# Layer 1's head and the fourth maximum of layers 1 and 3 moved in a four-layer attention kernel; semaphores cleared by five engines

## The chip, the cores and the metric

The kernel runs on one core of one Trainium2 chip. The metric is the device time of one execution in microseconds (us); lower is better. The kernel before takes 4179.82 us in the median of three runs (4173.48 to 4180.5).

## What is computed

Four attention layers in a row on a batch of four, each with tensors of 512 tokens by 512 features in float32. Cut to what matters:

```
x = L0(x, ctx)          # layernorm, 16 heads of 32, softmax, projection, GELU MLP
x = L1(x, ctx, mask)    # 32 query heads of 16 on 8 key heads, additive 512x512 mask, layernorm behind
x = L2(x, ctx, mask)    # layernorm of ctx, 16 heads of 32, tanh-gated residual
x = L3(ctx, x, mask)    # x asks, concat(ctx, x) of 1024 keys answers, rmsnorm, GELU MLP
# in each: scores = q @ k.T (scaled, masked); attn = softmax(scores); out = attn @ v
```

## The kernel before, in words

One loop runs over the four batch elements; its body computes all four layers for one element with everything in on-chip memory. The body's work is a hand-written list, `STEPS`, built layer by layer in `layer_steps` (lines 99 to 184). Every engine walks the same list and takes the steps that concern it, so the list's order is the order of each engine's instructions; counting semaphores hold the engines together.

**Steps.** `q` and `k` project 128 features and split the result in a high and a low part (two ScalarE instructions, lines 937 to 944, one GpSimd subtraction, line 646), which SyncE's queue stacks into one operand by 2 to 4 transfers of 256 KB each (line 600). Both parts' buffers are used again by the next `q` or `k`: ScalarE may write them only when the last stacking has landed. `max` multiplies one block of queries with all 512 keys (TensorE line 779) and VectorE takes each row's maximum (line 1075 in layer 1, where the mask is added on the way; line 1078 in layer 3). `maxT` transposes a unit's maxima (line 790), VectorE splits them (lines 1089, 1090), and two small transfers write them as rows of the query operand (line 607); only then may that unit's first `score` start. `score` computes two banks of transposed scores (line 807; in layer 1 with two more matmuls each that add the mask, lines 810 and 811), ScalarE takes the exponential (line 950), `pv_half` and `pv` multiply the probabilities with values and with ones (lines 848 and 850; line 827 in layer 1). `heads` closes a unit: ScalarE and VectorE fetch numerators and sums (VectorE lines 1103 to 1120). A unit is a group of four heads; layer 1 has eight units of four key tiles, layer 3 four units of eight key tiles, in two halves of 512 keys. `emax` is the form of `max` that computes two blocks at once in the score banks ahead of the attention; `part` is one of the four pieces of a projection between which emaxes are put.

**Two ring banks.** Everything but scores and pv results goes through two PSUM banks in turn (`RING = 2`): a ring step may start on TensorE when the step two before it has been taken away by VectorE or ScalarE (`take_ring`).

**The order around the change.** In the attention part the list goes group by group, one group for each key tile of a unit. Each group holds two scores of the next group, its own pv, and a share `part` of the maxima of later units (`late`, spread by a running count, or in layer 3 by the table `plan`):

```
steps += part[0:1] + ahead[0:1] + part[1:2] + ahead[1:2] + part[2:3]
steps += ([("pv_half", n, u, kt)] if n != 1 else []) + [("pv", n, u, kt)]
if kt == L.kt - 1:
    steps.append(("heads", n, u))
steps += part[3:]
```

So three filling steps stand ahead of pv and the fourth (and a fifth) behind pv and behind `heads`. `k(3,3,0)` and `k(3,3,1)`, the last keys of layer 3, are the fourth step of their groups.

**End of an iteration.** Behind the loop body SyncE clears 43 semaphores one after the other (lines 1144, 1145), then all engines meet at a barrier (line 1146) and the next iteration starts.

Of the kernel before, what the change touches and what calls it, by code (L numbers as in the profile page):

```python
# [34 lines left out]
NT = S // P  # L35
NC = D // P
# [43 lines left out]
def in_parts(main, between, first):  # L80

    out, pieces, gap = [], iter(between), 0
    for step in main:
        for c in range(NC):
            out.append(("part", step, c) if c < NC - 1 else step)
            gap += 1
            if gap > first:
                out += next(pieces, [])
    return out + [s for piece in pieces for s in piece]


def spread(steps, first, last):

    count = last - first + 1
    cuts = [len(steps) * i // count for i in range(count + 1)]
    return {first + i: steps[cuts[i]:cuts[i + 1]] for i in range(count)}


def layer_steps(L):

    n = L.n
    pairs = [(u, j, t, h) for u in range(L.units) for j in range(4) for t in range(0, NT, 2) for h in range(L.halves)]

    def closes(u, j, t, h):
        return [("maxT", n, u)] if (j, t, h) == (3, NT - 2, L.halves - 1) else []

    def early(count):
        return [[("emax", n, *p)] + closes(*p) for p in pairs[:count]]

    def late(count):  # L110
        out = []
        for u, j, t, h in pairs[count:]:
            out += [("max", n, u, j, t, h), ("max", n, u, j, t + 1, h)] + closes(u, j, t, h)
        return out

    def q(u):
        return ("q", n, u)

    def k(u, h=0):
        return ("k", n, u, h)  # L120

    def v(t, layer=n):
        return ("v", layer, t)

    if n == 0:
        done = 16
        steps = [("ctxT", c) for c in range(NC)] + [("norm", 0, "x"), v(0), k(0), v(1)] + [("xT", 0, "z", c) for c in range(NC)]
        steps += in_parts([q(0), k(1), q(1), v(2), v(3), q(2), k(2), q(3), k(3)], early(done), 17)
    elif n == 1:
        done = 12  # L130
        steps = [("maskT", 0), ("maskT", 1)] + [("xT", 1, "x", c) for c in range(NC)] + [q(0), ("maskT", 2), ("maskT", 3)]
        steps += in_parts([q(1)] + [v(t, 3) for t in range(NT)], early(done), 8)
    elif n == 2:
        done = 16
        steps = [("aT", c) for c in range(NC)] + [("norm", 1, "out"), k(0), v(0), v(1)]
        steps += [("xT", 2, "x", c) for c in range(NC)]
        steps += in_parts([q(0), k(1), v(2), q(1), v(3), k(2), q(2), k(3), q(3)], early(done), 16)
    else:
        done = 32
        steps = [k(0)] + [("xT", 3, "x", c) for c in range(NC)]  # L140
        steps += in_parts([q(0), k(0, 1), q(1), v(4), k(1), v(5), k(1, 1), q(2), v(6), k(2), q(3), v(7), k(2, 1)], early(done), 18)
    groups = [(u, kt) for u in range(L.units) for kt in range(L.kt)]
    fill = late(done)
    span, gone = len(groups) - L.kt - 2, 0
    plan = None
    if n == 3:
        two = fill.index(("maxT", 3, 2)) + 1
        plan = {}
        for part, first, last in ((fill[:two], 3, 13), (fill[two:], 15, 22)):
            plan.update(spread(part, first, last))  # L150
        plan[L.kt - 1] = plan[L.kt - 1] + [k(3)]
        plan[L.kt + 3] = plan[L.kt + 3] + [k(3, 1)]
    for pair in (2, 3) if n == 1 else ():
        fill.insert(len(fill) * 8 * (pair - 1) // span + 1, q(pair))
    steps += [("score", n, 0, 0), ("score", n, 0, 1)]
    for g, (u, kt) in enumerate(groups):
        upto = min(len(fill) * (g + 1) // span, len(fill))
        part, gone = fill[gone:upto], upto
        if plan is not None:
            part = plan.get(g, [])  # L160
        ahead = [("score", n, *divmod(2 * (g + 1) + i, L.slots)) for i in range(2)] if g + 1 < len(groups) else []
        steps += part[0:1] + ahead[0:1] + part[1:2] + ahead[1:2] + part[2:3]
        steps += ([("pv_half", n, u, kt)] if n != 1 else []) + [("pv", n, u, kt)]
        if kt == L.kt - 1:
            steps.append(("heads", n, u))
        steps += part[3:]
    steps += [("o", n, t) for t in range(NT)]
    if n in (0, 3):
        steps += [("norm", n, "mid")]
        if n == 0:  # L170
            steps += [("k", 1, 0, 0)] + [v(t, 1) for t in range(NT)]
        steps += [("xT", n, "mid", c) for c in range(NC)]
        if n == 0:
            steps.append(("ctx_in",))
        for f in range(NFB):
            steps += [("up", n, f, m) for m in range(NC)]
            if f:
                steps.append(("down", n, f - 1))
            if n == 0 and f == 1:
                steps.append(("norm", 2, "ctx"))  # L180
        if n == 0:
            steps.append(("mask_in",))
        steps += [("down", n, NFB - 1), ("mlp_out", n)]
    return steps


STEPS = [s for L in LAYERS for s in layer_steps(L)]
RINGED = ("ctxT", "xT", "aT", "maskT", "v", "q", "k", "max", "maxT", "o", "up")
RING_STEPS = [s for s in STEPS if s[0] in RINGED]
# [32 lines left out]
def build(nc, A, out):  # L222
    ctx = ExitStack()

    def sb(name, shape, dt=F32):
        return ctx.enter_context(nc.sbuf_tensor(name, shape, dt))
# [6 lines left out]
    with ctx:  # L233
        sems = []

        w = sb("w", [P, WSLOTS, NC, D])
        x = sb("x", [P, NT, D])
        ctxT = sb("ctxT", [P, NC, S])
        xT = sb("xT", [P, NC, S])
        at = sb("at", [P, NC, S])  # L240
        v = sb("v", [P, 8, D])
# [9 lines left out]
        maskT = ks[:, 2]  # L251
# [280 lines left out]
        with nc.Fori(0, B) as b:  # L532
# [608 lines left out]
                                nc.vector.tensor_tensor(x[:, t, :], score_banks[:, t, :], x[:, t, :], ALU.add  # L1141
                                                        ).then_inc(mlp_done, 1)

            for s in sems:
                nc.sync.sem_clear(s)
            nc.all_engine_barrier()

        with nc.Block() as block:
# [69 lines left out]
```

## Time and profile before

| | |
|---|---|
| median of three runs | 4179.82 us |
| the profiled execution | 4177.0 us, of which 4175.2 us are the span of its instructions |
| TensorE busy | 3729.6 us (89%) |
| VectorE, ScalarE, GpSimd busy | 1525.7 (37%), 1184.9 (28%), 293.5 us (7%) |
| mean granted TensorE clock | 0.955 |
| iterations start at | 26.4, 1059.6, 2107.3 and 3140.3 us |

Read the table so: TensorE does matmul work nearly always, so the time is made of its work, of the stretches in which it waits, and of the stretches in which its clock is granted at half (0.5, that is 1.2 instead of 2.4 GHz). Within iteration 0 layer 1 runs from 298.9 us (its head to 346.3, its attention to 540.7), layer 3 from 697 us (its attention from 776.9 to 912.6).

### The profile page before, as it was taken

Reading aid. Unit: us, or ns where it says so; the run is one execution under the profiler, and the core shown is the slowest. Engines: PE = TensorE matmul, PEld = TensorE weight load, DVE = VectorE, ACT = ScalarE, POOL = GpSimd, SP = SyncE. Lnnn points to the kernel's source line nnn. Section 1 sums busy time; section 2 is a strip of 40 time slices with the busy share of each in tenths; the row PEclk is TensorE's granted clock in tenths of the full one; section 3 lists DMA queues with packets and bytes.
Section 4 is the critical chain, followed back from the end, with each engine's and each line's share of the span. In section 5 each row is a group of like instructions: output and inputs, shape, how many; then the busy total and the mean of one; then the engine's idle time right before and its main releaser. Section 6 shows DMA issues by size and latency. Waiting matters only on the chain. (4 is left out here: it accounts for less than half of the span.)

```text
span 4175.2 us, 39552 instructions
## 1 busy us (share of the span) xinstructions
PE 3729.6 (89%) x14128; PEld 1791.6 (43%) x14128; DVE 1525.7 (37%) x2784; ACT 1184.9 (28%) x1404; POOL 293.5 (7%) x228
## 2 busy tenths in 40 slices
PE   6998899989899889998989988999897998989989
PEld 3444543434344554343434455434343445544434
DVE  3405543530330554353044055435304315443530
ACT  2312333331231232333123123233302312323330
POOL 3000011000100001100010000110001000011000
PEclk9999999999899899998999999999899999999999
DMA  7222154402523115340262311535025231163402
GB/s 141 66 82 40 21 89 65 74 24 93 95 62 91 32 21 91 60 75 25 86 103 62 91 32 21 101 55 84 11 98 90 72 89 23 21 107 52 81 11 101
DMA packets 153873, 275.29 MB, mean 66 GB/s; under 512 B 15584, under 2 KB 22436, under 8 KB 153656
## 3 DMA queue, kind: packets, MB, share of 16 engines
q1 hardware_dynamic: 153668, 272.55, 32.0%
q8 instruction: 130, 2.13, 0.2%
q14 instruction: 75, 0.61, 0.1%
HBM read 157.15 MB, written 4.19 MB: 39 GB/s over the span
## 5 line engine op out<-in xcount | busy, mean ns | idle before, releaser
L950 ACT ACTIVATE pt<-score_banks 128x1024 f32<-128x1024 f32 x768 | 763.8, 1023 | 956.9 <-PE score_banks L811 546.4
L682 PE MATMUL bank<-xT,w 128*128 128x512 f32 x1664 | 753.6, 599 | 36.1 <-ACT xT L923 23.2
L807 PE MATMUL score_banks<-qs,ks 99*128 99x512 f32 (+1 forms) x1280 | 445.8, 426 | 44.5 <-DMA qs<-nm_lo 27.4
L1078 DVE TENSOR_REDUCE mcol<-bank 128x1 f32<-128x512 f32 x512 | 348.3, 689 | 364.0 <-PE bank L779 358.5
L682 PEld LDWEIGHTS bank<-xT,w 128*128 128x128 f32 x1664 | 314.5, 192 | 388.1 <-issue 367.6
L880 PE MATMUL score_banks<-w,wide 128*128 128x512 f32 x1024 | 443.4, 592 | 0.0
L1075 DVE CUSTOM_DVE_ANT_0 bank<-bank,wide 128x512 f32<-128x512 f32 x416 | 286.7, 704 | 306.1 <-PE bank L779 305.6
L1061 DVE TENSOR_REDUCE mcol<-score_banks 128x2 f32<-128x1024 f32 x256 | 311.2, 1223 | 205.6 <-PE score_banks L770 188.0
L779 PE MATMUL bank<-ks,qs 97*128 97x512 f32 (+1 forms) x768 | 329.5, 449 | 61.0 <-DVE mcol L1078 30.5
L807 PEld LDWEIGHTS score_banks<-qs,ks 99*128 99x128 f32 (+1 forms) x1280 | 242.9, 197 | 182.9 <-ACT pt L950 71.3
L1140 DVE TENSOR_TENSOR score_banks<-score_banks,r_down 128x512 f32<-128x512 f32 x32 | 22.4, 700 | 800.4 <-PE score_banks L880 800.4
L880 PEld LDWEIGHTS score_banks<-w,wide 128*128 128x128 f32 x1024 | 194.6, 190 | 244.9 <-issue 244.9
L848 PE MATMUL bank<-pt,v 128*32 128x512 f32 x2048 | 289.2, 638 | 0.0
L770 PE MATMUL score_banks<-ks,qs 97*128 97x512 f32 x512 | 270.4, 610 | 11.9 <-issue 10.8
L850 PE MATMUL bank<-pt,ones 128*32 128x512 f32 x2048 | 278.6, 617 | 0.0
L779 PEld LDWEIGHTS bank<-ks,qs 97*128 97x128 f32 (+1 forms) x768 | 140.9, 193 | 302.1 <-issue 266.8
L968 ACT ACTIVATE wide<-bank,c_up 128x512 f32<-128x512 f32 x128 | 88.0, 687 | 577.6 <-PE bank L682 577.6
L862 PE MATMUL bank<-w,at 128*128 128x512 f32 x512 | 228.3, 599 | 10.9 <-POOL at L658 10.9
L810 PE MATMUL score_banks<-ks,ident_r 128*128 128x512 f32 x512 | 215.2, 420 | 0.0
L811 PE MATMUL score_banks<-ks,ident_r 128*128 128x512 f32 x512 | 214.7, 419 | 0.0
L658 POOL TENSOR_TENSOR at<-at,rden 128x512 f32<-128x512 f32 x64 | 81.4, 1271 | 1744.2 <-DVE rden L1120 1744.2
L737 PE MATMUL bank<-w,ctxT 128*128 128x512 f32 (+1 forms) x384 | 158.9, 545 | 41.9 <-ACT q_full L937 19.9
(112 smaller groups left out, 2924.1 us busy)
## 6 DMA issues: line engine op xcount, KB each, us to landing
ks<-k_high SPq DMA_DIRECT2D x136, 256.0 KB, 5.6
w<-in_up SPq DMA_DIRECT2D x32, 1024.0 KB, 5.1
w<-in_down SPq DMA_DIRECT2D x32, 1024.0 KB, 5.3
qs<-q_high SPq DMA_DIRECT2D x112, 256.0 KB, 6.9
ks<-k_full SPq DMA_DIRECT2D x72, 256.0 KB, 7.1
w<-in_v SPq DMA_DIRECT2D x17, 1024.0 KB, 5.3
w<-in_q SPq DMA_DIRECT2D x16, 1024.0 KB, 5.5
qs<-q_full SPq DMA_DIRECT2D x64, 256.0 KB, 6.5
```

The costliest lines, as they stand in the source:

```text
L682: last = nc.tensor.matmul(o[:, :], wt[:, c, cols[0]:cols[1]], src[:, c, :], start=(c == 0), stop=(c == NC - 1))
L770: last = nc.tensor.matmul(early_bank(e)[:, a, :], q_of(g)[0:L.row + 1, j, (t + a) * P:(t + a + 1) * P], k_of(g, h, kh)[0:L.row + 1, :], st ...
L779: nc.tensor.matmul(o[:, :], q_of(g)[0:L.row + 1, j, t * P:(t + 1) * P], k_of(g, h, kh)[0:L.row + 1, :], start=True, stop=True).then_inc(ri ...
L807: last = nc.tensor.matmul(o, k_of(g, kt // NT, kh)[0:L.row + 3, kt % NT * P:(kt % NT + 1) * P], q_of(g)[0:L.row + 3, j, :], start=True, st ...
L848: nc.tensor.matmul(num[rows, :], v_at(n, kt)[:, f0:f0 + 32], p_, start=kt == 0, stop=kt == L.kt - 1)
L850: last = nc.tensor.matmul(den[rows, :], ones[:, :], p_, start=kt == 0, stop=kt == L.kt - 1)
L862: last = nc.tensor.matmul(o[:, :], at[:, c, t * P:(t + 1) * P], wt[:, c, :], start=(c == 0), stop=(c == NC - 1))
L880: last = nc.tensor.matmul(score_banks[:, t, :], wide[:, f % 2, m, t * P:(t + 1) * P], wt[:, m, :], start=(f == 0 and m == 0), stop=(f == N ...
L950: nc.scalar.activation(pt[:, i % PTB], score_banks[:, 2 * (i % 2):2 * (i % 2) + 2, :], ACT.Exp, scale=L.scale).then_inc(exp_done, 1)
L1061: nc.vector.tensor_reduce(mcol[:, g % 2, h, 4 * j + t:4 * j + t + 2], early_bank(e), AX.X, ALU.max).then_inc(emax_done, 1)
L1075: nc.vector.tensor_tensor_reduce(bank[:, :], bank[:, :], wide[:, 0, t, :], 1.0, LOWEST, ALU.add, ALU.max, col).then_inc(free_of(step), 1)
L1078: ins = nc.vector.tensor_reduce(col, bank[:, :], AX.X, ALU.max)
```

## The change

Three edits:

1. Layer 1's head: the four mask transposes (`maskT`) stand together ahead of those of x. Before, two stood ahead and two behind `q(1,0)`. `q(1,0)` is now also cut in parts, and the first emax comes behind the third part of `v(3,0)`, where it came behind the first of `v(3,1)`.
2. In layers 1 and 3 all of a group's filling steps from the third on (`part[2:]`) stand ahead of pv, none behind it. In layer 3 the table's ranges end one group earlier: 3 to 12 and 14 to 21, where they were 3 to 13 and 15 to 22. With that `k(3,3,0)` and `k(3,3,1)` come ahead of the pv of their group.
3. The 43 semaphores are cleared by the five engines in turn: nine by each of SyncE, VectorE and ScalarE, eight by each of GpSimd and TensorE.

```
--- before.py
+++ after.py
@@ -128,8 +128,8 @@
         steps += in_parts([q(0), k(1), q(1), v(2), v(3), q(2), k(2), q(3), k(3)], early(done), 17)
     elif n == 1:
         done = 12
-        steps = [("maskT", 0), ("maskT", 1)] + [("xT", 1, "x", c) for c in range(NC)] + [q(0), ("maskT", 2), ("maskT", 3)]
-        steps += in_parts([q(1)] + [v(t, 3) for t in range(NT)], early(done), 8)
+        steps = [("maskT", c) for c in range(NC)] + [("xT", 1, "x", c) for c in range(NC)]
+        steps += in_parts([q(0), q(1)] + [v(t, 3) for t in range(NT)], early(done), 10)
     elif n == 2:
         done = 16
         steps = [("aT", c) for c in range(NC)] + [("norm", 1, "out"), k(0), v(0), v(1)]
@@ -146,7 +146,7 @@
     if n == 3:
         two = fill.index(("maxT", 3, 2)) + 1
         plan = {}
-        for part, first, last in ((fill[:two], 3, 13), (fill[two:], 15, 22)):
+        for part, first, last in ((fill[:two], 3, 12), (fill[two:], 14, 21)):
             plan.update(spread(part, first, last))
         plan[L.kt - 1] = plan[L.kt - 1] + [k(3)]
         plan[L.kt + 3] = plan[L.kt + 3] + [k(3, 1)]
@@ -159,11 +159,11 @@
         if plan is not None:
             part = plan.get(g, [])
         ahead = [("score", n, *divmod(2 * (g + 1) + i, L.slots)) for i in range(2)] if g + 1 < len(groups) else []
-        steps += part[0:1] + ahead[0:1] + part[1:2] + ahead[1:2] + part[2:3]
+        steps += part[0:1] + ahead[0:1] + part[1:2] + ahead[1:2] + (part[2:] if n in (1, 3) else part[2:3])
         steps += ([("pv_half", n, u, kt)] if n != 1 else []) + [("pv", n, u, kt)]
         if kt == L.kt - 1:
             steps.append(("heads", n, u))
-        steps += part[3:]
+        steps += [] if n in (1, 3) else part[3:]
     steps += [("o", n, t) for t in range(NT)]
     if n in (0, 3):
         steps += [("norm", n, "mid")]
@@ -1141,8 +1141,8 @@
                                 nc.vector.tensor_tensor(x[:, t, :], score_banks[:, t, :], x[:, t, :], ALU.add
                                                         ).then_inc(mlp_done, 1)
 
-            for s in sems:
-                nc.sync.sem_clear(s)
+            for i, s in enumerate(sems):
+                (nc.sync, nc.vector, nc.scalar, nc.gpsimd, nc.tensor)[i % 5].sem_clear(s)
             nc.all_engine_barrier()
 
         with nc.Block() as block:
```

**TensorE, layer 1's head**, before (L724 are mask transposes, L717 those of x, L682 with xT is `q(1,0)` and `q(1,1)`, L737 is values of layer 3, L770 is emax):

```order
L724 MATMUL bank<-ident,wide 128x128 x8
L717 MATMUL bank<-ident,x 128x128 x16
L682 MATMUL bank<-xT,w 128x512 x4
L724 MATMUL bank<-ident,wide 128x128 x8
L682 MATMUL bank<-xT,w 128x512 x4
L737 MATMUL bank<-w,ctxT 128x512 x5
L770 MATMUL score_banks<-ks 128x512 x2
```

and now:

```order
L724 MATMUL bank<-ident,wide 128x128 x16
L717 MATMUL bank<-ident,x 128x128 x16
L682 MATMUL bank<-xT,w 128x512 x8
L737 MATMUL bank<-w,ctxT 128x512 x3
L770 MATMUL score_banks<-ks 128x512 x2
```

Eight mask transposes moved from behind `q(1,0)` to ahead of x's, and two of the value matmuls from ahead of the first emax to behind it.

**TensorE, layer 1, end of unit 5** (L779 is max, L827 is pv; behind this pv VectorE runs `heads(1,5)`), before:

```order
654 L779 MATMUL bank4<-ks,qs 128x512
655 L827 MATMUL bank6<-pt,vone 32x512 x4
656 L779 MATMUL bank5<-ks,qs 128x512
657 L779 MATMUL bank4<-ks,qs 128x512
658 L807 MATMUL score_banks<-qs,ks 128x512
```

and now:

```order
654 L779 MATMUL bank4<-ks,qs 128x512
655 L779 MATMUL bank5<-ks,qs 128x512
656 L827 MATMUL bank6<-pt,vone 32x512 x4
657 L779 MATMUL bank4<-ks,qs 128x512
658 L807 MATMUL score_banks<-qs,ks 128x512
```

One max moved from behind pv to ahead of it; which bank each uses has not changed.

**TensorE, layer 3, the last maxima of unit 2** (L779 is max, L790 maxT, L807 score, L848 and L850 pv_half and pv), before:

```order
1050 L807 MATMUL score_banks<-qs,ks 128x512 x2
1051 L790 MATMUL bank5<-ident,mcol 16x128
1052 L848 MATMUL bank6<-pt,v 32x512 x4
1053 L850 MATMUL bank7<-pt,ones 32x512 x4
1054 L807 MATMUL score_banks<-qs,ks 128x512 x4
1055 L848 MATMUL bank6<-pt,v 32x512 x4
1056 L850 MATMUL bank7<-pt,ones 32x512 x4
1057 L779 MATMUL bank4<-ks,qs 128x512
1058 L807 MATMUL score_banks<-qs,ks 128x512 x2
```

and now:

```order
1046 L779 MATMUL bank4<-ks,qs 128x512
1047 L790 MATMUL bank5<-ident,mcol 16x128
1048 L848 MATMUL bank6<-pt,v 32x512 x4
1049 L850 MATMUL bank7<-pt,ones 32x512 x4
1050 L807 MATMUL score_banks<-qs,ks 128x512 x4
1051 L848 MATMUL bank6<-pt,v 32x512 x4
1052 L850 MATMUL bank7<-pt,ones 32x512 x4
1053 L779 MATMUL bank4<-ks,qs 128x512
1054 L807 MATMUL score_banks<-qs,ks 128x512 x2
```

The maxT of unit 2 (L790) went ahead by a pair of scores and a pv. The first max of unit 3 (row 1057 before, 1053 now), the first reader of both halves of `k(3,3)`, now stands ahead of scores 14 and 15 of unit 1; before, it stood behind them and a pv, directly ahead of unit 2's first score (row 1058). In the same way the maxT of unit 3 now stands two pvs and a pair of scores ahead of unit 3's first score; before, it stood directly ahead of it.

## Rows read from the trace of the kernel before

**Rows 1.** The page's busy time of TensorE, its share of the span, instructions
```profile
PE 3729.6 (89%) x14128; PEld 1791.6 (43%) x14128; DVE 1525.7 (37%) x2784; ACT 1184.9 (28%) x1404; POOL 293.5 (7%) x228
```

**Rows 2.** Cores view: span and mean granted TensorE clock
```profile
core 0: 4175.2 us, clock 0.955
```

**Rows 3.** Windows, layers 1 and 3: from:to length, PE, PEld, DVE, ACT, POOL busy, PEclk, DMA
```profile
346.30:540.70 194.40, 173.91 (x768) 103.72 (x768) 91.22 (x242) 71.00 (x72) 6.38 (x5) 0.94 0.12 22
776.90:916.40 139.50, 128.36 (x723) 51.94 (x724) 51.69 (x82) 65.67 (x70) 7.67 (x6) 0.95 0.16 26
...
2429.00:2619.20 190.20, 169.77 (x768) 101.52 (x768) 91.13 (x242) 71.00 (x72) 6.39 (x5) 0.96 0.13 22
```

**Rows 4.** Waits, TensorE, layer 1's attention: us in total, times, longest (346 to 541 us)
```profile
PE bank L779 <- DVE mcol L1075: 9.1, 8, 2.6
PE bank L790 <- issue: 4.5, 5, 0.9
PE bank L790 <- DVE mcol L1075: 2.4, 2, 1.3
...
PE bank L682 <- DVE mcol L1075: 1.2, 1, 1.2
...
PE bank L779 <- DMA ks<-q_full: 2.0, 1, 2.0
```

**Rows 5.** Timeline, TensorE, layer 1, end of unit 5: start, us, what [idle before <-releaser]
```profile
501.49 1.07 PE L827 MATMUL bank<-pt,vone 128*32 128x512 f32 x8
502.49 0.73 PE L779 MATMUL bank<-ks,qs 65*128 65x512 f32 x2
505.82 0.77 PE L779 MATMUL bank<-ks,qs 65*128 65x512 f32 x1 [2.60 <-DVE mcol L1075]
```

**Rows 6.** Timeline, VectorE, same place
```profile
502.62 0.72 DVE L1103 STREAM_TRANSPOSE denT<-bank 128x512 f32<-128x512 f32 x1 [0.27 <-PE bank L827]
...
504.33 0.70 DVE L1120 STREAM_TRANSPOSE rden<-rec 128x512 f32<-128x512 f32 x1
504.96 0.67 DVE L1075 CUSTOM_DVE_ANT_0 bank<-bank,wide 128x512 f32<-128x512 f32 x1
```

**Rows 7.** Waits, TensorE, layer 3's attention of iteration 0 (777 to 912 us)
```profile
PE score_banks L807 <- DMA qs<-nm_lo: 6.2, 2, 3.1
PE bank L779 <- DVE mcol L1078: 2.5, 7, 1.4
PE bank L790 <- DVE mcol L1082: 1.7, 2, 1.1
```

**Rows 8.** Timeline, TensorE, layer 3, second half of the fourth keys
```profile
824.06 3.70 PE L682 MATMUL bank<-xT,w 128*128 128x512 f32 x8
...
835.92 1.20 PE L807 MATMUL score_banks<-qs,ks 99*128 99x512 f32 x4
...
838.91 0.50 PE L779 MATMUL bank<-ks,qs 97*128 97x512 f32 x1
842.45 1.00 PE L807 MATMUL score_banks<-qs,ks 99*128 99x512 f32 x2 [3.04 <-DMA qs<-nm_lo]
```

**Rows 9.** DMA issues with median us to landing, 829 to 842 us
```profile
ks<-k_full SPq DMA_DIRECT2D x1, 256.0 KB, 6.8
```

**Rows 10.** Timeline, SyncE's queue, same place
```profile
831.83 0.61 SPq L600 DMA_DIRECT2D ks<-k_full  x1
```

**Rows 11.** Timeline, TensorE, layer 1's head
```profile
301.22 2.60 PE L717 MATMUL bank<-ident,x 128*128 128x128 f32 x16 [1.24 <-DVE ks L1036]
304.70 3.67 PE L682 MATMUL bank<-xT,w 128*128 128x512 f32 x8 [0.89 <-ACT xT L923]
...
323.17 2.05 PE L737 MATMUL bank<-w,ctxT 128*128 128x512 f32 x2 [4.95 <-ACT q_full L937]
```

**Rows 12.** Timeline, ScalarE, layer 1's head
```profile
322.34 0.69 ACT L937 ACTIVATE q_full<-bank,bq 128x512 f32<-128x512 f32 x1 [11.60 <-DMA ks<-q_full]
```

**Rows 13.** The line of the semaphore clears, around the end of iteration 0
```profile
L1145 SPq EVENT_SEMAPHORE_RANGE_CLEAR  x43: 25/25/49, 1052.7 to 1055.5; - x43
```

More of the change, by code:

```diff
@@ L130, in layer_steps @@
         done = 12
-        steps = [("maskT", 0), ("maskT", 1)] + [("xT", 1, "x", c) for c in range(NC)] + [q(0), ("maskT", 2), ("maskT", 3)]
-        steps += in_parts([q(1)] + [v(t, 3) for t in range(NT)], early(done), 8)
+        steps = [("maskT", c) for c in range(NC)] + [("xT", 1, "x", c) for c in range(NC)]
+        steps += in_parts([q(0), q(1)] + [v(t, 3) for t in range(NT)], early(done), 10)
     elif n == 2:
@@ L148, in layer_steps @@
         plan = {}
-        for part, first, last in ((fill[:two], 3, 13), (fill[two:], 15, 22)):
+        for part, first, last in ((fill[:two], 3, 12), (fill[two:], 14, 21)):
             plan.update(spread(part, first, last))
@@ L161, in layer_steps @@
         ahead = [("score", n, *divmod(2 * (g + 1) + i, L.slots)) for i in range(2)] if g + 1 < len(groups) else []
-        steps += part[0:1] + ahead[0:1] + part[1:2] + ahead[1:2] + part[2:3]
+        steps += part[0:1] + ahead[0:1] + part[1:2] + ahead[1:2] + (part[2:] if n in (1, 3) else part[2:3])
         steps += ([("pv_half", n, u, kt)] if n != 1 else []) + [("pv", n, u, kt)]
@@ L165, in layer_steps @@
             steps.append(("heads", n, u))
-        steps += part[3:]
+        steps += [] if n in (1, 3) else part[3:]
     steps += [("o", n, t) for t in range(NT)]
@@ L1142, in _ @@
                                                         ).then_inc(mlp_done, 1)
-            for s in sems:
-                nc.sync.sem_clear(s)
+            for i, s in enumerate(sems):
+                (nc.sync, nc.vector, nc.scalar, nc.gpsimd, nc.tensor)[i % 5].sem_clear(s)
             nc.all_engine_barrier()
```

## The prediction, written before the result

> **What bounds the kernel now.** I read the page first, then the cores, the windows of the two layers that the change touches, the waits inside them, and the timelines at each long wait. TensorE is busy for 89% of the span [rows 1]. So a step that it need not do does not exist here; what can be won is its waiting, and its clock. The mean granted clock is 0.955 [rows 2]: the missing 0.045 of 4175 us is 188 us of clock. Layer 1's attention has windows of 0.94 and 0.96 with 194.4 and 190.2 us, layer 3's one of 0.95 with 139.5 us [rows 3]; of layer 1's two, with the same work, the one with the lower clock is the longer. In layer 1 the waits are on VectorE, which empties the two ring banks: 9.1 us in 8 waits before a max, 2.4 and 4.5 us in 7 waits before a maxT, 1.2 us before `q(1,2)`, and 2.0 us on a stacking transfer [rows 4]. In layer 3 two waits of some 3 us each are on the rows of maxima (nm_lo), 6.2 us together, and 2.5 and 1.7 us on VectorE [rows 7]. The change reorders exactly these. I cost one iteration and multiply by four; the trace repeats these waits in each iteration.
>
> **Layer 1, maxima and heads.** Where a unit ends, pv is followed by two or three maxima while VectorE is still at `heads`. The longest case: maxima at 502.49, the next only at 505.82 after 2.60 us of waiting [rows 5], since VectorE transposes and adds from 502.62 to 505.03 and takes the first max only at 504.96, for 0.67 us and a read-out until 505.67 [rows 6]. With the fourth max ahead of pv, the banks that the steps behind pv need were emptied before `heads` began, and a pair of scores with their mask matmuls follows before the third step, which hides `heads`. By the order this takes away five waits: four of the 8 (their sum is 6.3 of the 9.1 us; the other four are about 0.7 us each, where three maxima stand in a row) and the 1.2 us before `q(1,2)`, 7.5 us together. Given back: at the ends of units 2 and 5 three maxima in a row now stand ahead of pv, 0.7 us each as in the four that stay, and 0.3 us behind `heads(1,5)`. Net 5.8 us.
>
> **Layer 1, maxT.** It waits 0.9 us behind the last max of its unit, 1.05 to 1.3 in two cases [rows 4]. In units 1, 3, 4, 5 and 6 pv (1.0 us [rows 5]) now lies between, and the wait falls to some 0.3 us; in units 2 and 7 two maxima stand right ahead of it and it grows by some 0.55. What goes in units 3 and 5 is not won: right behind these maxTs TensorE waits for `q(1,2)` and `q(1,3)` to be stacked (2.0 us in the first case [rows 4]), a chain of fixed length, so that wait grows by what is saved in front of it. Units 1, 4 and 6 give 1.95, units 2 and 7 take 1.1: net 0.9 us. Layer 1's attention wins 6.7 us.
>
> **Layer 1, head.** x's transposes start at 301.22 now [rows 11]. Two more mask transposes ahead of them each need a high copy on ScalarE and a subtraction on VectorE: some 1.9 us. The projection at 304.70 shifts by this, and with it the split and stacking of `q(1,0)`, on which ScalarE waits until 322.34 [rows 12] and TensorE, at half clock afterwards, until 323.17 [rows 11]. What the two mask transposes occupy between the projections is in the shadow of this chain, so moving them off there wins nothing. Against the 1.9 us: the first emax no longer has a value matmul ahead of it (1.0 us in the trace: half of 2.05). I take 1.0 us lost; bounds are 0 and, if the longer idle stretch keeps the clock at half through the first emaxes, 4.
>
> **Layer 3.** The waits of 3.04 us before `score(3,2,0)` at 842.45 [rows 8] and 3.1 before `score(3,3,0)` [rows 7] go: both maxTs now have two pvs and scores between them and the score. What is late next is `k(3,3,1)`. It starts at 824.06 and its last stacking transfer, issued at 831.83 [rows 10], needs 6.8 us [rows 9], until 838.6, 14.5 us after it. Its first reader stands at 838.91 [rows 8], just behind. Now a pair of scores (1.1 us: 835.92 to 837.05, the row behind [rows 8] follows at once), two maxima (0.6) and a bank wait no longer lie between, and 0.5 of a longer maxT wait is added: about 13.0 us, so a new wait of 1.5 us. The maxT waits, 1.7 us in two [rows 7], become 1.1 and 1.45, since maxima stand directly ahead: 0.85 lost. `heads(3,0)` was covered by `k(3,3,0)` behind its pv; now two short scores follow it, and the third max waits some 1.1 us (the 1.4 in rows 7 is the same case behind `heads(3,1)`, and it stays about as long, split in two). The two `k` steps behind a max of their bank: 0.7. Three groups with four maxima instead of three: 1.0 for two maxima in a row. A wait of 0.3 behind the `k` steps goes. Sum: -6.2 + 1.5 + 0.85 + 1.1 + 0.7 + 1.0 - 0.3 = -1.3 us.
>
> **The clock.** Half clock follows the long waits in the trace: TensorE runs at half after the wait of 4.95 us in the head (two matmuls in 2.05 us [rows 11]), the two matmuls behind the 3.04 us wait take 1.00 where four took 1.20 before [rows 8], the max behind the 2.60 us wait takes 0.77 where two took 0.73 [rows 5]. At 0.94 layer 1's attention loses 12 us (0.06 of 194.4), layer 3's at 0.95 7 us. The long waits on VectorE go and the stacking waits stay or grow; I take a quarter of layer 1's loss and two fifths of layer 3's, 3 us each. Bounds: 0 and 6 each.
> The Trainium skill ("TensorE: Matmul & The Clock Gate", Part 1, on the HAM clock gate) says that for modelling the ramp penalty is below 1% of a typical kernel's span. That would be under 42 us here, and this trace shows 188 us. By that rule the clock term would be 6 times 42/188, 1.3 us an iteration instead of 6, and the total 4138 us. The trace decides; its clock is a property of this kernel.
>
> **The clears.** SyncE's 43 clears start between 1052.7 and 1055.5 [rows 13]: 0.065 us each, although one lasts 0.025. Nothing lies beside them; all engines wait at the barrier. With nine it is 0.6 us if the others clear as fast: 2.2 us won. If another engine needs five times as long for one, nothing is won. I take 2.2.
>
> **Sum.** 6.7 + 3 - 1.0 + 1.3 + 3 + 2.2 = 15.2 us an iteration, 61 us in four. The profiled execution took 4177.0 us (span 4175.2), so 4116; the median of the runs is 2.8 us above it: 4119 us. The bounds of the terms (clock 0 to 12, head 0 to 4, layer 3 half gone or doubled, clears 0 to 2.2) give 4085 to 4158.
>
> **Rivals.**
> *The transfers end last.* The savings come ahead of stacking waits that absorb them: everything up to `q(1,2)` and `q(1,3)`, in layer 3 everything ahead of `k(3,3,1)`, and the longer idle stretches at the head and at `k(3,3,1)` take back the clock. For it: the three or four transfers of 256 KB take most of the distance already [rows 9, 10]. Against it: `heads(1,2)`, `heads(1,4)` and `heads(1,5)` lie behind these waits. Left are the clears and two or three waits, 4 us an iteration: 4164 us.
> *Slower: the fourth max stands waiting for its bank ahead of pv.* Place: every group of layer 1 with four filling steps, 26 of them. Two maxima in a row now come ahead of pv, and if VectorE has not emptied the bank of the max one pair of scores earlier, TensorE waits 0.7 us, as it does for three in a row, and pv and all behind it move. 26 times 0.7 is 18 us against 6.7 won: with the head, without a clock gain in layer 1 and with the rest as above 6 us an iteration lost, 4204 us. The point: emptying takes 0.8 us [rows 6] plus its start, the distance from the second to the fourth max is 1.9 us (two maxima of 0.25, a pair of scores 1.4). It decides if that becomes more than 1.9; after `heads` alone it does.
> *The change does nothing.* The other engines clear slowly, the waits change places: within 8 us of 4180.
>
> **Chances.** A measurement of this kernel can tell about 0.2% (8 us) from no change. Forecast 0.62, transfers last 0.19, nothing 0.08, bank waits 0.11. Faster by over 0.2%: 0.62 + 0.18 = 0.80; within 0.2%: 0.09; slower 0.11. The forecast's own range is 4085 to 4158; with the transfers' case it is 4083 to 4172, and the slower case and the tail are the 2 in 10 left out.
>
> **What would show it.** Right: the L779 waits on VectorE in layer 1's attention fall from 9.1 to 4 or 5 us, `q(1,2)`'s 1.2 is gone, the wait on ks<-q_full grows to 2.7; layer 3's waits on nm_lo are gone and one on ks<-k_full of 1 to 2 us is new; line 1145 takes 0.6 us on SyncE; the granted clock is above 0.955. Wrong: bank waits of 0.7 us at every group of layer 1, a head that is longer by over 3 us, a k wait of over 3 us, or a clock that stays.

## The result, and the profile after

The changed kernel takes 4057.22 us (median of 4 runs, 4051.81 to 4063.59), the kernel before 4176.65 us in its four: a ratio of 0.9723, 95% interval 0.9691 to 0.9755, so 119 us faster. The forecast was 4119 us, 58 us under the median given; the time lies below the range. The profiled execution took 4063.59 us, its span of 4061.8 is 113.4 us below that of before. One run of e6 (4481 us) and one of the kernel before (4266 us) fell in a slower state of the core; no ratio below uses them.

The page's line for TensorE, and the cores view:

```profile
PE 3664.7 (90%) x14128; PEld 1769.3 (44%) x14128; DVE 1524.0 (38%) x2784; ACT 1182.8 (29%) x1404; POOL 293.1 (7%) x228
```

```profile
core 0: 4061.8 us, clock 0.971
```

TensorE does the same 14128 instructions in 65 us less busy time than in [rows 1]; the clock rose from 0.955 [rows 2] to 0.971. As lost time that is 0.045 of 4175 = 188 us before and 0.029 of 4062 = 118 us now. **70 of the 113 us are clock**, 43 are the rest. The forecast had 24 and 37. TensorE's busy time says nearly the same in another way: 65 us less for the same instructions, and 48 us less of waiting.

The windows of iteration 0: layer 1's head, layer 1's attention, layer 2, layer 3's attention (columns as in [rows 3]), and then layer 0 and layer 2 of iteration 1:

```profile
298.90:348.00 49.10, 36.05 (x106) 19.14 (x104) 22.32 (x59) 8.59 (x13) 2.53 (x2) 0.86 0.41 65
348.00:528.70 180.70, 166.80 (x768) 100.77 (x767) 90.62 (x245) 70.93 (x72) 6.37 (x5) 0.97 0.14 25
544.00:681.00 137.00, 124.95 (x549) 56.85 (x548) 63.51 (x88) 51.27 (x64) 16.22 (x13) 1.00 0.46 78
760.30:894.10 133.80, 124.94 (x724) 50.54 (x722) 49.87 (x79) 67.69 (x73) 7.65 (x6) 0.97 0.19 39
```

```profile
1040.20:1308.60 268.40, 250.88 (x860) 115.29 (x861) 83.11 (x134) 66.24 (x84) 19.51 (x16) 0.97 0.39 85
1554.70:1691.60 136.90, 124.86 (x550) 56.86 (x549) 63.54 (x88) 51.26 (x64) 16.23 (x13) 1.00 0.46 78
```

The same two stretches of iteration 1, before:

```profile
1596.90:1738.40 141.50, 129.19 (x549) 58.29 (x548) 62.50 (x88) 51.38 (x64) 16.24 (x13) 0.96 0.44 76
1059.60:1335.10 275.50, 257.42 (x861) 118.47 (x862) 83.46 (x134) 66.97 (x84) 19.52 (x16) 0.95 0.38 83
```

Layer 1's attention went from 194.4 us at 0.94 to 180.7 at 0.97, layer 3's from 139.5 at 0.95 to 133.8 at 0.97 [rows 3]. (Layer 3's window stands 3.8 us later in rows 3 than here; the same steps took 139.6 us before too, from 773.0 to 912.6 us.) But layers 0 and 2, where the change moves nothing, gained too: layer 2 from 141.5 at 0.96 to 136.9 at 1.00, layer 0 from 275.5 to 268.4. Over all four iterations, from the clock record and the first TensorE instruction of each stage (the clock's part is half of the change in the time spent at 1.2 GHz; "busy" is the change in TensorE's busy time; all in us):

| stage | change | of it clock | the rest | busy | forecast clock / rest |
|---|---|---|---|---|---|
| layer 0 | -15.1 | -14.5 | -0.7 | -12.2 | 0 / 0 |
| layer 1, head | -4.0 | +1.7 | -5.7 | -3.9 | 0 / +4.0 |
| layer 1, attention | -49.8 | -22.2 | -27.6 | -24.0 | -12 / -26.8 |
| layer 2 | -14.5 | -15.4 | +0.9 | -13.4 | 0 / 0 |
| layer 3, head | +2.7 | +1.7 | +1.0 | +1.5 | 0 / 0 |
| layer 3, attention | -28.4 | -20.5 | -7.9 | -15.2 | -12 / -5.2 |
| layer 3, output and MLP, with the boundary | -4.3 | +0.3 | -4.6 | +2.3 | 0 / -8.8 |

The split by the clock record charges half clock even while TensorE stands idle. In layer 1's head that matters: more half clock falls into the longer wait, where it costs nothing, and the 4.0 us won there are all busy time, that is clock. In layer 3's attention the busy time gives 15 us to the clock and 13 to the waits.

The waits of TensorE in layer 1's attention of iteration 0, as in [rows 4]:

```profile
PE bank L779 <- DVE mcol L1075: 4.4, 7, 0.7
PE bank L790 <- DVE mcol L1075: 4.0, 6, 1.3
PE bank L779 <- DMA ks<-q_full: 2.8, 1, 2.8
PE bank L779 <- DMA qs<-q_full: 2.3, 2, 1.6
```

The waits before a max on VectorE fell from 9.1 us in 8 to 4.4 us in 7, none over 0.7, and `q(1,2)`'s 1.2 us is gone. The stacking wait grew from 2.0 to 2.8 us; the one on `q(1,3)` grew from 1.0 to 1.6 us.

The same in layer 3's attention, and the timeline at the fourth keys, to be held against [rows 7, 8]:

```profile
PE bank L779 <- DVE mcol L1078: 3.3, 10, 0.9
...
PE bank L779 <- issue: 1.2, 1, 1.2
PE bank L790 <- ACT pt L950: 1.1, 1, 1.1
PE bank L790 <- DVE mcol L1082: 1.1, 1, 1.1
```

```profile
824.70 1.04 PE L850 MATMUL bank<-pt,ones 128*32 128x512 f32 x8
826.90 0.47 PE L779 MATMUL bank<-ks,qs 97*128 97x512 f32 x1 [1.16 <-issue]
827.21 0.63 PE L807 MATMUL score_banks<-qs,ks 99*128 99x512 f32 x2
```

Both waits of 3 us on the rows of maxima are gone. In their place stands one of 1.16 us before the first max that reads `k(3,3)`, and 3.3 us in ten small ones. The profile names no releaser for the 1.16 us ("issue"); that it is the stacking of `k(3,3,1)` rests on e7 below, where this step begins one group earlier and the wait is gone in all four iterations.

Layer 1's head. Before, the long wait and the first emax behind it:

```profile
323.17 2.05 PE L737 MATMUL bank<-w,ctxT 128*128 128x512 f32 x2 [4.95 <-ACT q_full L937]
324.23 1.84 PE L770 MATMUL score_banks<-ks 65*128 65x512 f32 x2
```

Now:

```profile
303.50 3.68 PE L717 MATMUL bank<-ident,x 128*128 128x128 f32 x16 [0.81 <-DVE ks L1036]
...
325.45 1.22 PE L770 MATMUL score_banks<-ks 65*128 65x512 f32 x2 [7.71 <-DMA ks<-q_full]
...
340.63 0.28 PE L790 MATMUL bank<-ident,mcol 128*16 128x128 f32 x1 [1.50 <-DVE mcol L1057]
...
346.22 1.88 PE L737 MATMUL bank<-w,ctxT 128*128 128x512 f32 x4
348.23 0.47 PE L807 MATMUL score_banks<-ks 67*128 67x512 f32 x1
```

TensorE's long wait ends 2.28 us later (325.45 against 323.17) and is 7.71 us long, not 4.95; the first emax stands 1.22 us later (324.23 before), since no value matmul is ahead of it any more. The two emaxes at 325.45 take 1.22 us, about half clock as before [rows 11]. At the head's end `v(3,3)`'s last projections run up to `score(1,0,0)` at 348.23 (L807), which starts without a wait.

The clears by engine (three of the five; shortest/median/longest ns, first and last start), and SyncE's last store and next load around the end of iteration 0:

```profile
L1145 ACTq EVENT_SEMAPHORE_RANGE_CLEAR  x36: 41/41/41, 1035.1 to 4060.5; - x36
L1145 SPq EVENT_SEMAPHORE_RANGE_CLEAR  x36: 25/25/34, 1035.1 to 4060.4; - x36
...
L1145 PEldq EVENT_SEMAPHORE_RANGE_CLEAR  x32: 56/56/63, 1035.2 to 4060.9; - x32
```

```profile
1034.28 0.33 SPq L630 DMA_DIRECT2D out<-x  x1
1037.01 0.29 SPq L546 DMA_DIRECT2D m<-in_mask  x1
```

Nine clears for each engine (eight for two of them), side by side. The barrier is left 1.30 us after the first clear; with 43 on SyncE it was 3.06 us.

### The profile page after: what moved, and what is told of

It is laid out like the page before. It is cut to its first block and busy times, and to the rows that moved or that the text cites. A ratio compares the mean times of both kernels' runs of the same rounds, so it can differ in the third digit from the quotient of the medians.

```text
span 4061.8 us, 39552 instructions
## 1 busy us (share of the span) xinstructions
PE 3664.7 (90%) x14128; PEld 1769.3 (44%) x14128; DVE 1524.0 (38%) x2784; ACT 1182.8 (29%) x1404; POOL 293.1 (7%) x228
## 5 line engine op out<-in xcount | busy, mean ns | idle before, releaser
L682 PE MATMUL bank<-xT,w 128*128 128x512 f32 x1664 | 754.9, 600 | 26.5 <-ACT xT L923 23.1
L682 PEld LDWEIGHTS bank<-xT,w 128*128 128x128 f32 x1664 | 315.5, 192 | 381.2 <-issue 364.1
L807 PE MATMUL score_banks<-qs,ks 99*128 99x512 f32 (+1 forms) x1280 | 432.3, 415 | 19.5 <-ACT pt L950 16.6
L779 PE MATMUL bank<-ks,qs 97*128 97x512 f32 (+1 forms) x768 | 324.7, 439 | 59.0 <-DVE mcol L1078 33.3
L807 PEld LDWEIGHTS score_banks<-qs,ks 99*128 99x128 f32 (+1 forms) x1280 | 235.5, 191 | 158.9 <-ACT pt L950 73.5
L848 PE MATMUL bank<-pt,v 128*32 128x512 f32 x2048 | 280.1, 619 | 0.2
L770 PE MATMUL score_banks<-ks,qs 97*128 97x512 f32 x512 | 267.8, 605 | 13.0 <-issue 11.4
L850 PE MATMUL bank<-pt,ones 128*32 128x512 f32 x2048 | 271.9, 603 | 0.0
L779 PEld LDWEIGHTS bank<-ks,qs 97*128 97x128 f32 (+1 forms) x768 | 144.3, 190 | 290.3 <-issue 246.6
L810 PE MATMUL score_banks<-ks,ident_r 128*128 128x512 f32 x512 | 207.4, 405 | 0.0
L811 PE MATMUL score_banks<-ks,ident_r 128*128 128x512 f32 x512 | 207.3, 405 | 0.0
L1103 DVE STREAM_TRANSPOSE denT<-bank 128x512 f32<-128x512 f32 x80 | 57.3, 716 | 366.6 <-PE bank L850 272.9
```

The costliest lines, as they stand in the source:

```text
L682: last = nc.tensor.matmul(o[:, :], wt[:, c, cols[0]:cols[1]], src[:, c, :], start=(c == 0), stop=(c == NC - 1))
L770: last = nc.tensor.matmul(early_bank(e)[:, a, :], q_of(g)[0:L.row + 1, j, (t + a) * P:(t + a + 1) * P], k_of(g, h, kh)[0:L.row + 1, :], st ...
L779: nc.tensor.matmul(o[:, :], q_of(g)[0:L.row + 1, j, t * P:(t + 1) * P], k_of(g, h, kh)[0:L.row + 1, :], start=True, stop=True).then_inc(ri ...
L807: last = nc.tensor.matmul(o, k_of(g, kt // NT, kh)[0:L.row + 3, kt % NT * P:(kt % NT + 1) * P], q_of(g)[0:L.row + 3, j, :], start=True, st ...
L848: nc.tensor.matmul(num[rows, :], v_at(n, kt)[:, f0:f0 + 32], p_, start=kt == 0, stop=kt == L.kt - 1)
L850: last = nc.tensor.matmul(den[rows, :], ones[:, :], p_, start=kt == 0, stop=kt == L.kt - 1)
```

## The experiments

Each is held against the kernel before on the same chip, whose median was 4168 to 4175 us.

### The parts alone

**Only the clears** (e1), before with

```
-            for s in sems:
-                nc.sync.sem_clear(s)
+            for i, s in enumerate(sems):
+                (nc.sync, nc.vector, nc.scalar, nc.gpsimd, nc.tensor)[i % 5].sem_clear(s)
```

> The kernel before with only the semaphore clears spread over the five engines. Theory A (parts add up; each part is worth its own waits and the half clock that followed them; what layers 0 and 2 lost in the changed kernel came from nothing in particular but from where the clock's low stretches happened to fall): the barrier takes 1.3 instead of 3.06 us, 7 us in four iterations, and the half clock at the start of iterations 1 to 3 falls by 0 to 2 us each: 13 us faster, 4160 to 4170 us. Theory B (the gain in layer 0, 15 us in the changed kernel, belongs to the clears, since the idle stretch before the iteration is shorter): 22 us faster, about 4155 us, and layer 0 takes 267 to 268 us in iterations 1 to 3.

Measured: 0.9955 [0.9933, 0.9976], 19 us faster (10 to 28), between the two theories. Layer 0 takes 269.4, 271.5 and 267.1 us in iterations 1 to 3, against 275.5, 271.7 and 270.6.

**Only the head** (e2), the kernel before with the change's two lines for layer 1's first steps.

> The kernel before with only layer 1's head in the changed order. As first forecast: 1 us an iteration lost, 4 us slower, about 4181 us. As the changed kernel's trace reads (head 196.0 us in four iterations before, 192.0 after): 4 us faster, about 4173 us. In both the first emax comes behind an idle stretch of some 7.7 us. Theory A: layers 0 and 2 change by whatever the clock does there, in either direction, by up to 5 us an iteration.

Measured: 0.9963 [0.9939, 0.9987], 15 us faster (5 to 25); the interval excludes a loss. By the traces layer 1's head gives 5 us in four iterations and its attention 7.

**Only the fourth max of layer 1** (e3), `(part[2:] if n in (1,) else part[2:3])` ahead of pv.

> The kernel before with only layer 1's fourth filling step ahead of pv. Theory A: waits fall by 6.9 us an iteration and half clock costs 5.5 us less, 50 us faster, about 4127 us; layer 2 keeps its low stretches in most iterations. Theory B (layer 2's gain, 14 us, belongs to the denser end of layer 1's attention): layer 2 falls to 137 us in every iteration and the kernel to about 4113 us.

Measured: 0.9881 [0.9836, 0.9926], 50 us faster (31 to 68). Layer 2, in which this kernel has no instruction moved, runs at full clock in all four iterations (136.8 to 137.0 us); iteration 1:

```profile
1569.80:1706.60 136.80, 124.78 (x549) 56.86 (x548) 63.55 (x88) 51.30 (x64) 16.25 (x13) 1.00 0.46 78
```

**Only layer 3's part** (e4), the same with `n in (3,)` and the filling two steps shorter.

> The kernel before with only layer 3's edits (third and later steps ahead of pv, the table's ranges one group earlier). Theory A: waits fall by 2 us an iteration and half clock costs 5.1 us less, 28 us faster, about 4149 us. If most of that clock gain was chance: 8 to 15 us faster, about 4165 us. The new wait before the first max of unit 3 is 1.2 us and the one behind heads(3,0) 0.95 us in both.

Measured: 0.9933 [0.9911, 0.9955], 28 us faster (19 to 37); its attention takes 132.2 to 133.9 us, as in the changed kernel, while layer 2 stays at 141 to 142.

The four parts sum to 112 us, the change to 113 to 119: they add up as far as the intervals, 9 to 19 us either way, can tell. Layer 2's gain comes with layer 1's maxima.

### How one wait reaches layer 2

**The changed kernel with the group at the end of unit 5 as before** (e5):

```
+        ... (part[2:] if n in (1, 3) and (n, u, kt) != (1, 5, 3) else part[2:3])
+        steps += [] if n in (1, 3) and (n, u, kt) != (1, 5, 3) else part[3:]
```

> The changed kernel with one of its layer 1 groups as before: the third and fourth last steps of the last group of unit 5 stand behind pv and heads again, so the wait of 2.6 us some 50 us ahead of layer 2 is back in place of 0.7 us. Theory A (a low stretch of the clock costs only where it stands): 1.9 us of waiting and about 3.4 us of half clock an iteration, 21 us slower than the changed kernel in four, about 4080 us, layer 2 stays at 136.9 us. Theory B (a low stretch at the end of layer 1 brings another one about 50 us later, at the start of layer 2): layer 2 is back at 141 to 142 us in most iterations, 35 to 40 us slower than the changed kernel, about 4095 us.

Measured: 0.9756 [0.9723, 0.979], 14 us over the changed kernel (the intervals of the two overlap; the traces tell more). The 2.60 us wait is back, and layer 1's attention takes 183.7 to 186.8 us, 12 us more in four iterations; layer 2 stays at 136.9 in all four. So this wait costs some 12 us on the spot and nothing in layer 2: Theory B falls.

**The kernel before with that one group moved** (e6), the same condition with `== (1, 5, 3)`.

> The kernel before with only the last group of unit 5 in layer 1 in the changed order. Theory A: 1.6 us of waiting and 3.4 us of half clock an iteration, 20 us faster, about 4150 us, layer 2 stays at 141 to 142 us in most iterations. Theory B: layer 2 falls to 137 us in all four as well, 34 us faster, about 4136 us.

Measured: 0.9945 [0.9927, 0.9963], 23 us faster. Layer 2 is 141.7, 137.3, 136.8 and 140.3 us in its four iterations, with the same program in each. Iterations 0 and 1:

```profile
555.40:697.10 141.70, 129.18 (x550) 58.16 (x548) 62.47 (x88) 51.38 (x64) 16.23 (x13) 0.96 0.44 76
1596.90:1734.20 137.30, 124.99 (x549) 56.91 (x548) 63.53 (x88) 51.27 (x64) 16.23 (x13) 1.00 0.45 78
```

Whether layer 2 loses its clock is thus not fixed by the order of its steps.

**What fixes it is where layer 2's start falls.** In each trace's clock record all changes of the granted clock stand on one raster of even steps. I took the start of layer 2 in the four iterations of the twelve kernels without fillers between the layers, 48 starts in all. In 18 of them the clock falls to half within 4 us of the start, and these 18 are exactly the ones that start 0.05 to 0.43 us ahead of a raster time. The other 30 start elsewhere (the nearest at 0.00 and 0.70 us ahead) and have full clock there. The waits of layer 2's first steps (1.2, 0.5 and 1.1 to 1.2 us) are in all 48. So layer 2's 14 us come from a shift of its start by what stands ahead of it. In iteration 0 of e6 and in three iterations of e9 the clock falls there though there was no half clock in the 100 us ahead, so no earlier low stretch is needed.

**The kernel before, with the waits in layer 2's first steps filled** (e10): 22 transposes whose result nobody uses, into a bank that is free there, ahead of the last factor of `o(1,0)` (9) and among the steps of `aT` (9 and 4).

> The kernel before, with 22 transposes without use in three waits between layers 1 and 2 (9 in the wait of 1.2 us for the last factor of o(1,0), 9 and 4 in those of 1.24 and 0.52 us among the aT steps; written to a score bank that nothing reads). These waits are the same in the kernel before and the changed one, but layer 2 had 10 us of low stretches in three of four iterations before and none after. If these waits bring layer 2's half clock on: layer 2 takes 137 us in all four iterations, 10 to 14 us faster than before, about 4158 us. If layer 2's half clock comes from what lies further ahead: no change or up to 4 us slower.

Measured: 0.9974 [0.9952, 0.9997], 11 us faster (1 to 20). Layer 2 takes 137.3, 136.8, 138.3 and 138.4 us. The same place in iteration 1, first before (L717 are aT's transposes, the first L682 is the projection behind them), then filled (L720 and L682; the fillers are L715):

```profile
1598.77 1.07 PE L717 MATMUL bank<-ident,v 128*128 128x128 f32 x8 [1.24 <-DVE x L1132]
1600.36 0.97 PE L717 MATMUL bank<-ident,v 128*128 128x128 f32 x4 [0.52 <-ACT wide L923]
1602.39 6.12 PE L682 MATMUL bank<-wide,w 128*128 128x512 f32 x8 [1.07 <-ACT wide L923]
```

```profile
1586.08 1.15 PE L715 MATMUL score_banks<-ident,ctxT 128*128 128x128 f32 x9
1587.40 1.09 PE L720 MATMUL bank<-ident,v 128*128 128x128 f32 x8 [0.17 <-DVE x L1138]
...
1590.65 3.67 PE L682 MATMUL bank<-wide,w 128*128 128x512 f32 x8 [1.07 <-ACT wide L929]
```

The idle of 1.24 us shrinks to 0.17, the 0.52 goes, the 1.07 stays, and the same eight matmuls take 3.67 us in place of 6.12. But three of this kernel's four starts of layer 2 fall outside the 0.05 to 0.43 us ahead of a raster time, where the clock stays full without fillers too. Only the one of iteration 2 lies inside (0.21 us), and there the clock held until some 65 us later. That is one case in favour of the short waits being needed, and the run does not show more.

### The clears, seen from the other side

**The changed kernel with all clears on SyncE** (e11), as before.

> The changed kernel with the clears on SyncE alone again. By the barrier alone (3.06 instead of 1.30 us) 7 us slower than the changed kernel, 4064 us; with the half clock at the iteration's start as in the run of the clears alone, which was 19 us faster than before: 4070 to 4076 us.

Measured: 0.9796 [0.9762, 0.983], 30 us over the changed kernel, more than expected. Its layer 0 of iteration 1, and TensorE's restart there, then the restart in the changed kernel:

```profile
1041.10:1321.70 280.60, 260.83 (x861) 119.33 (x862) 83.48 (x134) 66.85 (x84) 19.53 (x16) 0.94 0.38 82
```

```profile
1041.11 3.77 PE L717 MATMUL bank<-ident,v 128*128 128x128 f32 x16 [9.33 <-issue]
1045.62 5.66 PE L737 MATMUL bank<-w,ctxT 128*128 128x512 f32 x8 [0.73 <-ACT ctxT L894]
```

```profile
1040.23 3.77 PE L717 MATMUL bank<-ident,v 128*128 128x128 f32 x16 [7.58 <-issue]
1044.74 3.67 PE L737 MATMUL bank<-w,ctxT 128*128 128x512 f32 x8 [0.73 <-ACT ctxT L894]
```

After an idle of 9.33 us the eight L737 take 5.66 us at half clock, after 7.58 us they take 3.67. Layer 0 takes 280.6 us at 0.94 against 268.4 at 0.97. Over the four iterations layer 0 gives 22 of the 34 us between the two profiled executions, and all of it is clock (half clock for 94.5 us against 49.2, half of the difference 22.6).

One pair of restarts proves little, so here are all of them, three in each of the fourteen kernels. With the clears on five engines the idle is 7.3 to 8.0 us, and the eight L737 take 3.67 us in 21 of 21. With the clears on SyncE it is 9.1 to 9.9 us, and they take 5.5 to 6.2 us in 13 of 21 and 3.67 in the other 8; one of these 8 is in the kernel before, iteration 3:

```profile
3140.26 3.49 PE L717 MATMUL bank<-ident,v 128*128 128x128 f32 x16 [9.10 <-issue]
3144.48 3.67 PE L737 MATMUL bank<-w,ctxT 128*128 128x512 f32 x8 [0.73 <-ACT ctxT L894]
```

Here too the raster decides among equals: the 13 restart 0.54 to 2.04 us behind a raster time, the 8 elsewhere. None of the 21 restarts behind the shorter idle falls into that range, so the runs do not separate the length of the idle from its place. What they show is the sum: layer 0 of iterations 1 to 3 takes 810 to 825 us in the seven kernels with all clears on SyncE (mean 818) and 802 to 812 in the seven others (mean 806). These 12 us and the barrier's 7 are the 19 of e1.

SyncE's first load is late as well:

```profile
1040.50 0.29 SPq L546 DMA_DIRECT2D m<-in_mask  x1
```

It starts 6.3 us after the first clear (1034.2); in the changed kernel 1.9 us after it (1035.1 to 1037.01). No run shows that TensorE pays for this: it restarts 6.9 and 5.2 us after the first clear, and the 1.7 us between are those of the barrier.

### What is left in the changed kernel

**The chains of the stacked queries and keys begun earlier** (e7):

```
-        plan[L.kt + 3] = plan[L.kt + 3] + [k(3, 1)]
+        plan[L.kt + 2] = plan[L.kt + 2] + [k(3, 1)]
-        fill.insert(len(fill) * 8 * (pair - 1) // span + 1, q(pair))
+        fill.insert(len(fill) * 8 * (pair - 1) // span - 3, q(pair))
```

> The changed kernel with q(1,2) and q(1,3) four filling steps earlier and k(3,3,1) one group earlier, so that their stacking starts sooner. The three waits on stacking (2.76, 1.62 and 1.16 us in the changed kernel) go, 22 us in four iterations; if the half clock behind them (10 us of low stretches or more an iteration) goes too, another 20 to 30 us: 4005 to 4020 us. Rival: stacking cannot start sooner because its buffers are free only behind unit 1's and unit 3's last pv; then the waits shrink by less than 1 us each and the time is about 4050 us.

Measured: 0.9662 [0.9636, 0.9688], 4023.43 us, 34 below the changed kernel by the medians, 25 by the two ratios. Layer 1's attention of iteration 0, its window and waits:

```profile
351.00:522.70 171.70, 162.40 (x768) 98.40 (x768) 90.05 (x244) 70.94 (x72) 6.43 (x5) 1.00 0.14 26
```

```profile
PE bank L779 <- DVE mcol L1075: 4.8, 9, 0.7
PE bank L790 <- DVE mcol L1075: 4.0, 6, 1.3
PE bank L779 <- DMA ks<-q_high: 0.3, 1, 0.3
```

9.0 us less than the 180.7 of the changed kernel, at full clock throughout, though nine waits of up to 0.7 us and six of up to 1.3 us on VectorE stand there, where the changed kernel has seven and six. The two stacking waits (4.4 us) went, and with them 10.2 us of half clock, 5.1 us lost. Over four iterations the attention is 42 us shorter. In layer 3 the wait of 1.16 us before the first max of unit 3 is gone.

**The head's idle filled** (e8): the changed kernel with 48 transposes without use ahead of the first emax that waits for `q(1,0)`.

> The changed kernel with 48 transposes into a bank that is written again at once (work without use, some 6.5 us) put where TensorE waits 7.7 us for the stacking of q(1,0) in layer 1's head. Nothing is taken away and nothing made shorter. If half clock follows idle stretches and is what the head's low stretch of 7 to 13 us costs, that stretch goes: 3.4 to 5 us an iteration, 14 to 20 us faster than the changed kernel, about 4040 us. If the clock does not depend on this wait: the same, 4057 us; if the 48 take longer than the wait: slower by the excess.

Measured: 0.9698 [0.9673, 0.9722], 4042.09 us, 15 below the changed kernel by the medians, 10 by the ratios, whose intervals overlap. The head's window and timeline in iteration 0:

```profile
298.90:348.00 49.10, 40.89 (x161) 24.07 (x160) 22.73 (x60) 8.58 (x13) 2.54 (x2) 0.97 0.41 65
```

```profile
318.54 5.40 PE L764 MATMUL score_banks<-ident,ctxT 128*128 128x128 f32 x48
326.42 0.73 PE L774 MATMUL score_banks<-ks 65*128 65x512 f32 x2 [2.47 <-DMA ks<-q_full]
```

The first two emaxes take 0.73 us where they took 1.22, at 326.42 instead of 325.45; the window's clock is 0.97, not 0.86. But most of that half clock had stood in the wait itself: the head is only 3 us shorter in four iterations, not the 14 to 20 expected. The larger gain is layer 1's attention, 713.0 against 728.5 us, where no step and no wait differs and the half clock fell from 54.6 to 20.5 us; layer 0 lost 11 us. So the time came out as forecast, by luck, and from other stages than the one that was filled.

**Both** (e9).

> The changed kernel with both of the last edits that made it faster: stacking four steps (one group) earlier, and 48 transposes without use in the head's wait. If the two act in different places (149 us faster than before, and 130 us), they add: 4023 less 15, about 4008 us. If the low stretches that one of them spares come up elsewhere: 4015 to 4023 us.

Measured: 0.9613 [0.958, 0.9647], 4011.41 us: the fastest kernel here, 46 us below the changed one, nearly the 49 of the two gains together. Layer 2 loses its clock again in it (562.4 us in four iterations, 549.2 in e7).

**Both, and e10's fillers** (e12).

> The fastest kernel so far (stacking early and the head's wait filled, 4011 us) with the 22 transposes without use between layers 1 and 2 as well. Its trace has 10.2 us of low stretches in layer 2 in three iterations and 3.4 in the fourth, which the changed kernel had not. If filling the waits in front of them takes them away as it did in the kernel before (11 us faster there, layer 2's low stretches from 30.6 to 6.8 us in all): 13 to 17 us faster, about 3996 us. If the clock then falls elsewhere: 4005 to 4011 us.

Measured: 0.9634 [0.961, 0.9659], 4015.04 us: no gain over e9. Layer 2's half clock fell from 34 to 10 us, but the total over the program rose from 158.9 to 166.0: layer 0 has 21 us more of it and layer 3's attention 14.

## Why the prediction was wrong, and what held

**Direction and mechanism held, step by step.** Layer 1's waits came out where and as large as forecast: 4.4 us before the maxima (4 to 5), 2.76 on the stack (2.7), three maxima in a row 0.7, maxT 0.3 to 0.5 and 1.3 (0.3 and 1.45); all in all 27.6 us in four iterations against 26.8. Layer 3: the new k wait 1.16 us (1.5), the third max 0.95 twice (1.1), maxT 1.07 twice (1.1 and 1.45), two maxima in a row 0.19 (0.35): every small term was put a little high, which makes 7.9 us against 5.2 (13 by the waits themselves).

**The step that failed: "I take a quarter of layer 1's loss and two fifths of layer 3's, 3 us each."** Measured are 5.6 and 5.1 us an iteration there, in the two attentions that I looked at, both inside the bounds of 0 and 6. Outside the bounds is the place: layer 0 and layer 2 gave 30 us more, and I had costed them at nothing because the change does not touch them. Layer 2's 14 us hang on where its start falls by fractions of a microsecond, which no sum of waits could have told; as far as the forecast goes, they are luck. Layer 0's belong in the main to the clears. The clock term was 6 us an iteration and is 17.5. The view that would have warned me is the windows over the untouched stages: layer 2 has 137.2 us in iteration 0 and 141.5, 141.3 and 141.9 in the others, with the same instructions. A stage whose time differs between iterations loses something that can come back. The range has a slip of its own: its upper end leaves out the clears' term at 0, with which it would be 4166 and not 4158. The time missed the lower end.

**The Trainium skill** ("TensorE: Matmul & The Clock Gate", Part 1) puts the ramp penalty below 1% of a typical span, which gave 4138 us. All half clock in this case's traces is 4.5% of the span before (188 us) and 2.9% after. The sentence is about the ramp at a kernel's start; what costs here are stretches in its midst, so it should not have been set against them. By weighing the row higher I came nearer, and still took the loss for a local one.

**The clears** were a term of 2.2 us an iteration. The barrier gave 1.76 us (3.06 to 1.30), as TensorE's clears take 0.12 us each from start to start against SyncE's 0.066. What was not in the sum is what stands behind the long idle: e1 won 19 us and e11 lost 30 where the term says 9. That the engines wait at the barrier I had; that the restart's clock can differ with it (13 of 21 at half, against 0 of 21) I did not ask.

**The head** was forecast 1.0 us lost, and e2 shows 15 us won. The later chain was right (2.28 us against 1.9), and so was the value matmul taken off (the first emax is 1.22 us later, 0.9 in the sum). Missed was the other end: before, TensorE stood 2.07 us ahead of `score(1,0,0)` with nothing left to do, and now `v(3,3)`'s shifted projections fill this, and a maxT wait shrinks from 2.31 to 1.50 us; a stretch of half clock at the start of the attention, there before in all four iterations, is gone. I counted what the moved steps delay and not what they fill.

**The rivals.** That the transfers end last was half right: the stacking waits grew as said and hold 34 us (e7), but they gave back only what the sum had subtracted already. The slower case fell: of the seven waits left before a max in layer 1 six of 0.7 us are the rows of three, and the one at a mere pair ahead of pv is the 0.18 us behind `heads(1,5)`, forecast at 0.3. That the clears move nothing fell with e1.

**What stays open**: whether the length of the idle at the barrier matters beside its place (no restart after the shorter idle fell where the longer ones went to half clock), and whether the short waits are needed for layer 2's half clock (one case in e10). An echo at a fixed distance from a single wait is excluded by e5. Why the five kernels with layer 1's maxima moved and the stacking as it was (the changed kernel, e3, e5, e8, e11) have all twenty starts of layer 2 in the good range, and e9 three of four in the bad one, follows from the times of the steps ahead; no run tells if it would hold for another kernel.

## What to carry to other kernels

A wait of TensorE costs its length and the half clock that may follow, here about as much again in layer 1's attention (26 us of waits and 24 of busy time). Half clock also comes and goes in stages that the edit does not touch, since it depends on where they start: so compare the time and granted clock of equal stages over the iterations, before costing an edit at "waits only" and before crediting it with what an untouched stage won. Begin chains of split, copy and stacking so early that no matmul waits for them, and measure whether filling a wait that can't go pays (e8 gained, e12 did not). Spread what stands alone at a barrier over all engines, by the price of one on the slowest, and when steps are moved, look at what they fill as well as at what they delay.

## What the runs showed of the hardware that I had not expected

- Equal instructions in a stage cost 136.8 to 142.2 us, nearly all of it by the clock (layer 2, twelve kernels), and the kernel before, e1 and e6 have both within one execution. Which of the two it is went in 48 of 48 cases by where the stage's start fell against the raster of the clock's changes, to a few tenths of a microsecond.
- Transposes without use made the kernel faster: 48 in a wait of 7.7 us won 10 to 15 us in four iterations (e8), 22 in waits of about 1 us won 11 (e10, 1 to 20), both mostly in stages or at starts that the fillers only shifted.
- 43 clears in a row on SyncE are followed by a load 6.3 us after the first clear, nine by one after 1.9 us. The clears account for 2.8 and 0.5 us of it: some 2 us more pass after the long row. Why is open.
- A clear takes 0.12 us from start to start on TensorE, 0.085 on VectorE, 0.07 on ScalarE and GpSimd, and 0.057 on SyncE (0.066 with 43 in a row), though the durations listed are 25 to 56 ns.
